# One choice for the whole of layer 1's loop, another way of spreading c, and a new order of steps ahead of the loop

## The reference

```python
def _L1_gnn_ref(X, A, W, a):
    XW = jnp.matmul(X, W)
    s_col = jnp.matmul(XW, a[0, :f])
    s_row = jnp.matmul(XW, a[0, f:])
    Z1 = jax.nn.leaky_relu(s_row[:, None] + s_col[None, :], negative_slope=0.01)
    den = jnp.exp(Z1)
    num = jnp.matmul(A, den)
    att = jnp.where(num != 0, den / jnp.where(num != 0, num, 1.0), 0.0)
    return jnp.matmul(A, jnp.matmul(att, XW))
```

## Time and profile before

| | us |
|---|---|
| median of 3 runs | 727.4 (727.07 to 728.39) |
| the profiled execution | 728.87 |
| its span, first to last instruction | 727.1 |

### The profile page before, as it was taken

How to read it: one execution, slowest core, us unless ns; L and a number is a source line. 1 busy time by engine, 2 the same in 40 slices (tenths; PEclk the granted TensorE clock), 3 DMA queues, 4 the chain that set the end, 5 groups by cost and what they waited for, 6 DMA issues and landing times.

```text
span 727.1 us, 11809 instructions
## 1 busy us (share of the span) xinstructions
PE 596.3 (82%) x4179; PEld 345.3 (47%) x4179; DVE 576.3 (79%) x1043; ACT 445.5 (61%) x689; POOL 388.7 (53%) x456
## 2 busy tenths in 40 slices
PE   5499999999998779999526978878889878787994
PEld 5243333333332668888423643333444333345883
DVE  2589999999999863688786768887988988995442
ACT  2388888888888332679964227876766777741000
POOL 5458888877778224456207154464564543001764
PEclk9999999999999589999656998999999999997998
DMA  9964444490000000000000032233332322100110
GB/s 146 101 68 39 39 39 39 51 379 31 1 1 0 6 0 15 23 17 16 17 0 23 14 110 52 83 88 88 88 88 65 81 70 81 43 4 3 31 30 15
DMA packets 17841, 37.94 MB, mean 52 GB/s; under 512 B 2570, under 2 KB 8222, under 8 KB 17726
## 3 DMA queue, kind: packets, MB, share of 16 engines
q0 software_dynamic: 7392, 24.32, 19.6%
q1 hardware_dynamic: 10334, 11.98, 5.0%
HBM read 48.72 MB, written 10.45 MB: 81 GB/s over the span
## 4 chain that ended last, share of the span: by engine, by line
PE 34%; DVE 25%; issue 21%; POOL 12%; ACT 5%; DMA 1%; DVEq 0%; POOLq 0%; ACTq 0%; SPq 0%
DVE ring L825 8%; PE PSALL L1633 8%; DVE R L834 7%; PE PSALL L1388 5%; POOL AW L459 5%; PE PSALL L1501 3%; ACT AW L608 3%; PE PSALL L1618 3%; PE PSALL L1369 2%; POOL X L472 2%; PE PSALL L1319 2%; PE PSALL L1583 2%; POOL X L450 2%; PE PSALL L1447 1%; POOL iota L470 1%
## 5 line engine op out<-in xcount | busy, mean ns | idle before, releaser
L398 POOL TENSOR_TENSOR R<-R,ring 128x452 f32<-128x452 f32 (+1 forms) x126 | 151.6, 1204 | 33.2 <-ACT ring L536 31.5
L834 DVE SCALAR_TENSOR_TENSOR R<-ring,R 128x452 bf16<-128x452 f32 (+1 forms) x132 | 134.7, 1021 | 0.0
L1369 PE MATMUL PSALL<-R,AO 128*128 128x452 bf16 (+2 forms) x396 | 99.3, 360 | 16.1 <-DVE R L834 15.0
L459 POOL DMA_INDIRECT AW<-ATd,FR x44 | 50.4, 1146 | 106.9 <-PE PSALL L1585 81.7
L536 ACT ACTIVATE ring<-ring,sm 128x452 f32<-128x452 f32 (+1 forms) x132 | 88.4, 670 | 27.8 <-DVE ring L825 21.0
L1319 PE MATMUL PSALL<-XN 128*128 128x452 f16 (+2 forms) x396 | 99.3, 362 | 4.7 <-issue 4.2
L1583 PE MATMUL PSALL<-AW,R 128*128 128x452 fp8e4 x348 | 89.6, 359 | 7.2 <-DVE R L1167 3.7
L544 ACT ACTIVATE R<-ring,sm 128x452 bf16<-128x452 f32 (+1 forms) x132 | 88.6, 671 | 4.3
L1618 PE MATMUL PSALL<-ring,X 128*128 128x452 bf16 (+1 forms) x300 | 69.2, 366 | 19.5 <-issue 14.0
L825 DVE TENSOR_TENSOR ring<-PSALL,AT 128x452 f32<-128x452 f32 (+1 forms) x132 | 81.0, 614 | 0.9 <-PE PSALL L1319 0.9
L1369 PEld LDWEIGHTS PSALL<-R,AO 128*128 128x128 bf16 (+1 forms) x396 | 28.5, 97 | 76.2 <-DVE R L834 62.0
(11 more groups left out here) (256 smaller groups left out, 1033.6 us busy)
## 6 DMA issues: line engine op xcount, KB each, us to landing
AT<-in_adjT POOLq DMA_DIRECT2D x22, 338.5 KB, 6.5
ATd<-AT SPq DMA_DIRECT2D x2, 3723.5 KB, 17.3
XWd<-ring SPq DMA_DIRECT2D x11, 128.0 KB, 1.8
out<-ring SPq DMA_DIRECT2D x21, 64.0 KB, 1.5
AW<-ATd,FR POOLq DMA_INDIRECT x44
X<-XWd,idx POOLq DMA_INDIRECT x22, 3.8
Wt<-in_W SPq DMA_DIRECT2D x1, 64.0 KB, 10.8
X<-in_x SPq DMA_DIRECT2D x1, 0.5 KB, 7.6
```

Of the source, the lines that this page charges most:

```text
L398: i = G.tensor_tensor(ES_, ES_, z, ALU.add)
L459: G.indirect_dma_start(out=AW2[:, jt % 3, q, :], out_offset=None, in_=ATd, in_offset=bass.IndirectOffsetOnAxis(ap=idxw[:, q, jt:jt + 1], a ...
L834: V.scalar_tensor_tensor(F[0:rows, RW:RW + w], z, 1.0, F[0:rows, 0:w], ALU.subtract, ALU.subtract).then_inc(s_low, 1)
L1369: m = TE.matmul(PSALL[:, c, 0:w], half_[0:rows, jt, :], F[0:rows, o:o + w], start=(jt == 0 and k == 0), stop=(jt == T - 1 and k == 2))
```

## The change

Seven edits, all from the order of c on:

- GpSimd's `cdiag` products go, and so does `onesf`. `spread_c` multiplies, for each tile, a column of `c99` broadcast over 128 columns with the identity, so 22 products of 128 columns in place of 6 of up to 512. They stand ahead of the mask counts, groups 4 and 5 (banks 0 and 1) first.
- On VectorE the rank tile 20 comes behind the weights `w88`, next to rank tile 21; on TensorE column sums 20 and 21 come behind block sums 0; on ScalarE the copies of c come ahead of row sums 20 and 21.
- `thirds` is called ahead of `settle`.
- Three `empties` come behind parts 0 and three behind block sums 3, in banks 4, 5 and 7; `without_empty` follows them.
- `win` has one more value, whether any tile is wide. On each of TensorE, ScalarE and VectorE the loop of layer 1 stands twice: without the wide case under `If(any == 0)`, and in full under `Else`.
- In the copy without the wide case, TensorE does the sums over the first 128 rows for both halves, then under `If(kind == 1)` the second 128 rows for both, then the table's product for both. VectorE and ScalarE have no choice in it.
- Block sums 4 and parts 3 come behind pair 0's sums, block sums 5 and parts 4 behind pair 1's, and parts 5 ahead of pair 2's. The tables on VectorE and ScalarE follow, and so does the second `window_rows`.

```diff
-            for g, (t0, nb) in enumerate(GRP):
-                G.tensor_tensor(cdiag[g][:, 0:nb * P].rearrange("p (t j) -> p t j", t=nb),
-                                ident[:, :].unsqueeze(1).broadcast_to([P, nb, P]),
-                                c99[:, t0:t0 + nb].unsqueeze(2).broadcast_to([P, nb, P]), ALU.mult).then_inc(s_cdiag, 1)
...
+
+            def spread_out(n):
+
+                t0, nb = GRP[CORDER[n]]
+                av.wait_ge(s_cball, n + 1)
+                S.activation(cb[:, t0 * P:(t0 + nb) * P], PSALL[:, CBANK[CORDER[n]], 0:nb * P], ACT.Copy).then_inc(s_cbc, 1)
+
             av.wait_ge(s_sU, 1)
             S.activation(sU, sU, ACT.Exp).then_inc(s_eU, 1)
-            row_sum(0, T - 2)
+            spread_out(0)
+            spread_out(1)
             av.wait_ge(s_wU, 1)
             S.activation(w88[:, :, 0:T], wU, ACT.Copy).then_inc(s_whi, 1)
+            for n in range(2, 6):
+                spread_out(n)
+            row_sum(0, T - 2)
...
+                    if v == 0:
+                        table_high(3)
+                        sums_out(4)
...
+                    elif cp == 1 and jt + 1 < T:
+                        den_exp_small(jt + 1)
+                    if v == 1:
+                        sums_out(5)
+                        table_high(4)
+                        table_high(5)
...
+            reg["any"] = eng.value_load(win[0:1, 2 * T:2 * T + 1], min_val=0, max_val=1)
+            met = av.covered()
+            with eng.If(reg["any"] == 0):
+                layer1(False)
+            av.only(met)
+            with eng.Else():
+                layer1(True)
+            av.only(met)
...
+            split_ok = thirds(1)
             settle(1)
             hots(1)
-            valued(1, thirds(1))
+            valued(1, split_ok)
             places(1)
...
-            rank_steps([(0, T - 2)])
...
-            rank_steps([(0, T - 1)])
+            rank_steps([(0, T - 2), (0, T - 1)])
...
+            k = own.step(V.tensor_reduce(any_wide, widef, AX.X, ALU.max))
...
+                        else:
+                            if cp == 0:
+                                small_scores(jt + 1)
+                            if cp == 1:
+                                small_halves(jt + 1)
+                    if v == 0:
+                        table(3)
+                        window_rows(FIRST, T, 4)
+                    if v == 1:
+                        table(4)
+                        table(5)
+                attention_low(NV - 1)
...
             def spread_c(g):
+
                 t0, nb = GRP[g]
-                pe.wait_ge(s_cdiag, g + 1)
-                pe.wait_ge(s_gset, 6)
-                if g >= 4:
-                    pe.wait_ge(s_cbc, g - 3)
-                TE.matmul(PSALL[:, CBANK[g], 0:nb * P], onesf, cdiag[g][:, 0:nb * P], start=True, stop=True).then_inc(s_cball, 1)
+                pe.wait_ge(s_c99, 1)
+                pe.wait_ge(s_idxc, 1)
+                for q in range(nb):
+                    m = TE.matmul(PSALL[:, CBANK[g], q * P:(q + 1) * P], c99[:, t0 + q:t0 + q + 1].broadcast_to([P, P]),
+                                  ident[:, :], start=True, stop=True)
+                m.then_inc(s_cball, 1)
...
-            col_sums(0, T - 2)
+            for g in CORDER:
+                spread_c(g)
             pe.wait_ge(s_mask, 2)
             for t in range(T):
                 rows = rows_of(t)
                 m = TE.matmul(PSALL[:, 7, 64:64 + 2 * T], onesb[0:rows, :], mLU[0:rows, t, :], start=(t == 0), stop=(t == T - 1))
             m.then_inc(s_count, 1)
-            for g in range(4):
-                spread_c(g)
             block_sums(0)
+            col_sums(0, T - 2)
             col_sums(0, T - 1)
-            for g in (4, 5):
-                spread_c(g)
             block_sums(1)
             both_parts(0)
+            for c in range(3):
+                empties(c)
             block_sums(2)
             both_parts(1)
             ordered(0)
             block_sums(3)
+            for c in range(3, NC):
+                empties(c)
             both_parts(2)
...
+                else:
+                    small_sums(v, (0,))
+                    met = pe.covered()
+                    with eng.If(kinds[jt] == 1):
+                        small_sums(v, (1,))
+                    pe.only(met)
+                    table_sums(v)
...
+            def layer1(general):
+
+                for v in range(NV + LAG):
+                    if v == 2:
+                        both_parts(5)
+                    if v < NV:
+                        num(v, general)
+                    if v == 0:
+                        both_parts(3)
+                        block_sums(4)
+                    if v == 1:
+                        block_sums(5)
+                        both_parts(4)
+                    if v >= LAG:
+                        xw_product(v - LAG)
+
+            pe.wait_ge(s_win, WIN)
+            reg["any"] = eng.value_load(win[0:1, 2 * T:2 * T + 1], min_val=0, max_val=1)
+            met = pe.covered()
+            with eng.If(reg["any"] == 0):
+                layer1(False)
+            pe.only(met)
+            with eng.Else():
+                layer1(True)
```

More of the change, by code:

```diff
@@ L204, in adj_resnorm2_kernel @@
         sq, nrm, rn, deg, dis, rs, rrs, scol, srow, cs, _, _, l_w = (st[:, i, :] for i in range(13))
-        onesf, _, selr = (ring[:, q, 0:P] for q in range(3))
+        selr = ring[:, 2, 0:P]
         onesb = RF[:, 2180:2180 + P // 2].bitcast(BF16)
@@ L1198, in _ @@
             den_all(0)
[L1199 to L1209 removed]
+            for c in range(3, NC):
+                without_empty(c)
             def attention_scores(v):
@@ L1574, in num @@
                 pe.wait_ge(s_rbm, NC)
-                pe.wait_ge(s_tab, NC)
-                def sums_of(tiles):
-                    for h, (b, c0, w) in enumerate(pair):
-                        if v:
-                            pe.wait_ge(s_ln, 2 * v - 1 + h)
-                        for q in range(tiles):
-                            for part in (1, 0):
-                                TE.matmul(PSALL[:, b, 0:w], den_h[:, s + 1 + q, :, part], AW[:, jt % 3, q, c0:c0 + w],
-                                          start=(q == 0 and part == 1), stop=False)
-                        TE.matmul(PSALL[:, b, 0:w], den_h[:, s, :, 1], tab[:, c0:c0 + w],
-                                  start=False, stop=True).then_inc(s_num, 1)
@@ L1588, in num @@
-                met = pe.covered()
-                with eng.If(reg["kind"] == 0):
-                    sums_of(1)
-                pe.only(met)
-                with eng.If(reg["kind"] == 1):
-                    sums_of(2)
-                pe.only(met)
-                with eng.If(reg["kind"] == 2):
-                    for h, (b, c0, w) in enumerate(pair):
-                        if v:
-                            pe.wait_ge(s_ln, 2 * v - 1 + h)
-                        for t in range(T):
-                            for part in (1, 0):
-                                m = TE.matmul(PSALL[:, b, 0:w], den_h[:, t, :, part], AT[:, t, c0:c0 + w],
-                                              start=(t == 0 and part == 1), stop=(t == T - 1 and part == 0))
-                        m.then_inc(s_num, 1)
@@ L1604, in num @@
[L1604 to L1620 removed]
+                pe.wait_ge(s_tab, min(2 * v + 2, NC))
@@ new lines, in xw_product @@
+            def xw_product(p):
+                jt, high, lower = p // 3, *halves_of(p)
+                pe.wait_ge(s_alo, p + 1)
+                pe.wait_ge(s_xws, 3 * (jt + 1))
+                for q in range(2):
+                    c = 2 * (p % 3) + q
+                    part_of = slice(q * RW, q * RW + CH[c][1])
+                    for k, (part, att) in enumerate(((1, high), (1, lower), (0, high))):
+                        m = TE.matmul(PSALL[:, c, 0:CH[c][1]], XWh[:, jt, :, part], att[:, part_of],
+                                      start=(jt == 0 and k == 0), stop=(jt == T - 1 and k == 2))
+                m.then_inc(s_y, 1)
```

248 lines of the change are left out of this document (131 added, 117 removed).

## The result

The kernel after takes 707.45 us, median of 4 executions (705.56 to 707.68), against 727.24 us (726.84 to 728.39, 4 executions) of the kernel before: a ratio of 0.972, 95% interval 0.970 to 0.974. The profiled execution is the one of 705.56 us; its span is 703.8 us, against 727.1. It is the fastest of the four, by 1.7 us, while the profiled execution of the kernel before (728.87) lies above its median: the medians are 19.8 us apart, the two profiles 23.3. What follows explains the 23.3.

A forecast was written before the change was run, and what follows sets the result against it. TensorE was taken to bound the front from 388 to 430; in the loop neither TensorE nor VectorE was full, with TensorE stalling on jumps over code. 728.9 - 6.2 - 4.3 - 15.4 + 1.6 = 704.6 us, range 697 to 718.

The forecast's parts named there:

- Steps 1 to 3: Front: c spread by identity products, weights ahead of last ranks, TensorE's queue reordered; ordered(0) starts at 405.2, -6.2 us.
- Step 4: From ordered(0) into the loop: 26.1 us to pair 3's sums instead of 30.4, -4.3 us; bounds -6 and -1.
- A + 8: Pair 0's forecast start, 8 us after A, the end of ordered(0), set by the gather of tile 0.
- the bound of -1: Into the loop: the gain is only 1 us if TensorE falls to half clock while it waits.
- Step 5: Layer 1's loop: without wide code and its stalls, 60 pairs take 179.0 us instead of 194.4, -15.4 us.
- The worry about the cycle between TensorE and ScalarE: In the loop: cycle of 2.1 us plus the choice's cost, leaving 0.7 at a pitch of 2.8 to 3.1.
- Step 6: Behind the loop: each engine jumps over the general loop on leaving, +1.6 us; bounds 0 and 3.8.
- Rival B: The loop keeps its pitch, stalls not the jumps' or new order ties TensorE and ScalarE: 716.0 us, chance 0.22.
- D: Slower: the choice between sums and table's products stalls 1.92 us in every pair of kind 0: 758 us, chance 0.04.
- C: The front gives less: spreads at half clock (+2.9), half clock in first pairs (+3): 710.5 us, chance 0.13.

The follow-up runs named there:

- 88 products: Kernel after with 88 never-run products put behind a choice in every pair of TensorE's short loop, only jumped over: 724.54 us, loop 193.3.
- 44 products: Kernel after with 44 never-run products put behind a choice in every pair of TensorE's short loop, only jumped over: 704.99 us, loop 177.2.
- the kernel with the rank tile first: Kernel after with rank tile 20 ahead of the weights again on VectorE: 707.48 us.
- the two of the front: Two kernels built on after: GpSimd's diagonals brought back at the new place in the queue (707.35 us), and rank tile 20 ahead of the weights again (707.48 us).
- the jump at entry: Kernel after with the loop's two copies in the other order, so each engine jumps on entering the short loop, not on leaving: median 704.85 us, ratio 0.966.
- the third improved kernel: Kernel after with the choice turned round, block sums 4 and parts 3 ahead of pair 0, and ScalarE's Exp over r in six pieces: median 702.55 us.

## Why the prediction was right, and where it was off

The forecast of 704.6 stands on the profiled 728.9, so it is a gain of 24.3 us; for the median it means 703.1. Measured are 707.45 and a gain of 19.8 between the medians, 23.3 between the profiles. The mechanisms were right in the main. Of the 4.5 us that are missing between the medians, 1.0 is in the profiles; the rest the steps below can't place, since only the fastest execution of after has a trace. By steps, on the profiled execution:

- **Steps 1 to 3, the front up to ordered(0)**: -6.2 forecast, -7.3 measured (411.40 to 404.11). The spreads were to end at 388.1 and ended at 387.5, block 0 was to start at 389.2 and started at 388.12, because the clock rose before 385 (granted 0.79 from 383 to 385, where I had taken 385) and the counts took 0.74 instead of 1.1. From block 0 to ordered(0) it was to be 16.0 and is 15.99. That the masks shrink from 1.50 to 0.65 I had left out; it was not on the path.
- **Step 4, into the loop: the term that was mis-sized.** -4.3 forecast; from the end of ordered(0) to the sums of pair 3 it is 29.0 us against 30.4 before, so -1.4. Pair 0 starts at A + 8.5 (A + 8 forecast). I had it wait for the gather and left out VectorE's three late `without_empty`, which by the traces hold it as long or longer; the number was near because both end together, and that is luck. Behind the wait TensorE ran at half clock: pair 0 took 3.1 instead of 1.9 and the parts 1.2 instead of 0.8. I had this as the bound of -1 and took the better value; the earlier trace rows had shown the same fall at 433.6, so the row spoke for the bound. How much this costs differs between executions (below). Block 4, pair 1, block 5, the parts and the wait for the last table came as forecast (4.2 + 1.9 + 4.2 + 0.8 + 2.3 = 13.4; 418.24 to 431.68 is 13.44). The other 0.8 is pair 3's: behind the table wait ScalarE's Ln start afresh, and pair 3's sums wait 0.63 for them.
- **Step 5, the loop**: -15.4 forecast, -17.2 measured. Its bound was named rightly: TensorE's stalls go, and VectorE's 8.4 us of work a tile (168.18/20) sets the tiles of kind 0, TensorE those of kind 1. I had 8.76 and 9.3 a tile; they take 8.5 and 9.4, and one takes 10.8. The stalls were the skipped code's, as the 88 products show. The worry about the cycle between TensorE and ScalarE didn't come true in the sum, though the old order of the sums would have been 1.8 better.
- **Step 6, leaving the choice**: +1.6 forecast, +1.8 at the exit; 2.0 to the end of the span.

Sum: -7.3 - 1.4 + 0.6 - 17.2 + 2.0 = -23.3; the 0.6 that stands against it is between the sums and the scores of pair 3, which are 2.59 apart now and 2.03 before. Rival B fell with the loop's 177.2, and the kernel that has TensorE's full loop shows why; D fell with the one that has no choice, which was no faster. (D counts 48 pairs of kind 0; seven of the 22 tiles are of kind 1, so they are 45, and its 758 would be some 2 us less.) Half of C came true in the profile of after, in the first pairs but not in the spreads. In the kernel with 88 products, whose queue is the same there, the spreads ran at half clock as well, to 389.4.

Step 4 had a range that one profile doesn't show. In the kernel with 44 products, whose queue is the same up to the loop, the wait ahead of pair 0 is as long, but the granted clock stayed at 1.00 from 413 to 418:

```profile
413.49 1.69 DVE L1129 SCALAR_TENSOR_TENSOR R<-R,PSALL 128x452 f32<-128x452 f32 x3
...
415.44 1.69 PE L1625 MATMUL PSALL<-AW,R 128*128 128x452 fp8e4 x8 [2.98 <-DVE R L1129]
```

There pair 3's sums start 27.3 us behind ordered(0). It is 29.0 in after, and 30.2 in the kernel with the rank tile first, where the clock was at 0.50 up to 420. Against the 30.4 of before the step is worth -3.1, -1.4 and -0.2: with the clock held, 1.2 us of the 4.3 are missing, and the clock behind the wait takes another 1.7 to 2.9.

## What to carry to other kernels

Code that is jumped over is not always free (88 products a pair cost 16 us of the loop, 44 nothing): if the trace has idle time put down to "issue" behind a choice and instruction packets to go with it, hoist the rare case out of the loop, and let the common path be the one that is left straight on. A jump over a whole copy of the loop cost 1.1 to 4.1 us once, so put it where the engine waits anyway, at the entry more easily than at the exit. When a wait on TensorE stands ahead of work that bounds, price the work behind it at both clocks: behind 3.0 us of waiting it fell in six profiles and held in one. And before you believe what a wait is put down to, compare kernels: where two end 0.1 us apart, the one named can be the wrong one.

## What the runs showed that I had not expected

- **A threshold.** Skipping 44 products a pair costs nothing and 88 cost 16 us, though both are fetched in full. Its cause is open.
- **The place of a stall may count as much as its size.** 26 us of "issue" ahead of the direct sums made a loop of 202.0, 28.8 us of idle time ahead of the XW products 194.4. With 88 products, 26 us ahead of the table's products made one of 193.3. The blocks' order differs too, so this is a reading of the rows.
- **The clock's rise scatters.** With the same queue of work ahead of it, TensorE's granted clock rose at different times in these profiles. From 385 to 387 it was 1.00 in after, 0.50 in the kernel with 88 products, 0.50 and 0.50 in the two of the front, 0.79 in the jump at entry; TensorE was busy throughout. Block sums 0 start between 388.12 (after) and 390.15 (88 products), 2.0 us apart; the products of the ends started 0.5 apart already, so 1.5 us are the clock's. The executions of after lie as far apart (705.56 to 707.68), but all four have the same mean granted clock, 0.942, so that the clock makes their difference isn't shown. Of the third improved kernel two executions had a mean granted clock of 0.946 and 0.947 and took 700.28 and 700.80, two had 0.939 and took 704.30 and 704.47. Single executions can't tell changes of 2 us in this kernel; comparing the same marks in the traces can.
